# Turning tap-multiplied weights on TensorE, packing half of pair 0, and moving one tap and the bias add off VectorE

## What is computed

```python
x = x + L0(_gn(x))      # x is (16, 96, 16, 16); _gn: group norm, 32 groups of 3 channels
x = x + L1(_gn(x))
# L0: qkv = 1x1 convolution by w_qkv (288x96), then a depthwise 3x3 convolution by w_dw;
#     q and k are divided by their l2 norm over the 256 pixels; 8 heads of 12 channels:
#     attn = softmax(q k^T * temperature); out = w_proj (attn v)
# L1: s = softmax(x gate_w + gate_b) over 4 experts; the two largest are weighted by their softmax;
#     y[e] = w2[e] relu(w1[e] x + b1[e]) + b2[e]; out = sum over e of coef[e] * y[e]
#     coef[e] = sum over rank k of (expert e is at rank k for any pixel) * weight of rank k
```

## Time and profile before

| | us |
|---|---|
| median of 3 runs (168.86 to 171.39) | 170.21 |
| the profiled execution | 170.19 |
| its span, first to last instruction | 168.4 |
| PE busy | 148.9 |
| DVE busy | 144.0 |
| ACT busy | 101.4 |
| POOL busy | 45.4 |

### The profile page before, as it was taken

One profiled execution on the slowest core, in us unless ns is written; L12 is line 12 of the kernel. 1 busy time (PEld: TensorE's weight loads), 2 busy tenths in 40 slices (PEclk: granted clock), 3 DMA queues, 4 the chain that ended last, 5 costly groups with the idle time before them and its releaser, 6 DMA issues.

```text
span 168.4 us, 3554 instructions
## 1 busy us (share of the span) xinstructions
PE 148.9 (88%) x1275; PEld 118.6 (70%) x1275; DVE 144.0 (86%) x389; ACT 101.4 (60%) x227; POOL 45.4 (27%) x63
## 2 busy tenths in 40 slices
PE   0486896999998999999999899898999798999963
PEld 0476795999998999999999899675674242333322
DVE  2579999877999999999799699659779999999992
ACT  3075087565928639379399147485499768675710
POOL 5130220540514235425246225451227000000000
PEclk9999999699999999999999999999999999999999
DMA  6994305041140410503204100000000000112313
GB/s 151 226 232 103 70 0 157 6 134 26 38 124 0 133 29 0 155 9 85 76 2 117 44 0 6 0 0 2 4 0 0 0 0 0 47 47 58 90 47 93
DMA packets 8810, 9.72 MB, mean 58 GB/s; under 512 B 3640, under 2 KB 7512, under 8 KB 8792
## 3 DMA queue, kind: packets, MB, share of 16 engines
q1 hardware_dynamic: 8648, 9.25, 21.8%
q10 hardware_dynamic: 144, 0.24, 0.4%
HBM read 2.94 MB, written 1.57 MB: 27 GB/s over the span
## 4 chain that ended last, share of the span: by engine, by line
PE 44%; DVE 42%; issue 7%; DMA 2%; ACT 2%; POOL 1%; DVEq 0%; POOLq 0%
DVE v_acc L1136 9%; PE qk_ps L720 8%; PE qk_ps L722 8%; DVE h_mixed L1395 5%; PE out_ps L809 4%; DVE stats L1092 3%; PE sc_ps L774 3%; PE sc_ps L784 3%; PE qk_ps L725 3%; DMA x_sb<-in_x 2%; PE v_ps L766 2%; DVE wc L1021 2%; DVE x_sb L1403 2%; PE small_ps L826 2%; PE v_ps L969 2%
## 5 line engine op out<-in xcount | busy, mean ns | idle before, releaser
L1136 DVE SCALAR_TENSOR_TENSOR v_acc<-v_ps,v_taps,v_acc 96x576 f32<-96x576 f32 x64 | 51.8, 809 | 1.2
L720 PE MATMUL qk_ps<-w_a,x_a 128*128 128x192 f16 x243 | 46.6, 245 | 0.0
L722 PE MATMUL qk_ps<-w_b,x_b 128*128 128x192 f16 x243 | 46.5, 245 | 0.0
L720 PEld LDWEIGHTS qk_ps<-w_a,x_a 128*128 128x128 f16 x243 | 24.6, 101 | 0.2
L722 PEld LDWEIGHTS qk_ps<-w_b,x_b 128*128 128x128 f16 x243 | 23.6, 97 | 0.3
L527 ACT ACTIVATE h_mixed<-qk_ps,slope 128x512 f32<-128x512 f32 x24 | 16.9, 775 | 5.4 <-PE qk_ps L946 5.3
L725 PE MATMUL qk_ps<-w_c,x_c 96*128 96x192 f16 x81 | 20.1, 248 | 0.0
L479 ACT ACTIVATE sc_exp<-sc_qk,neg_max 96x12 f32<-96x12 f32 x16 | 4.7, 296 | 21.3 <-DVE neg_max L1175 21.3
L640 POOL TENSOR_TENSOR sq_sum<-qk_sq 128x384 f32<-128x384 f32 x8 | 8.0, 1002 | 32.8 <-ACT qk_sq L441 25.1
L1395 DVE TENSOR_TENSOR h_mixed<-h_mixed,hidden 128x512 f32<-128x512 f32 x24 | 15.0, 679 | 0.0
L1092 DVE BATCH_NORM_STATS2 stats<-x_sb 96x6 f32<-96x256 f32 x32 | 11.7, 412 | 3.0 <-DMA x_sb<-in_x 2.8
(11 more groups left out here) (200 smaller groups left out, 349.9 us busy)
## 6 DMA issues: line engine op xcount, KB each, us to landing
x_b<-x_a SPq DMA_DIRECT2D x7, 324.0 KB, 3.1
x_sb<-in_x SPq DMA_DIRECT2D x8, 192.0 KB, 4.8
out<-xs SPq DMA_DIRECT2D x7, 192.0 KB, 2.1
x_a<-x_lo SPq DMA_DIRECT2D x7, 108.0 KB, 2.7
x_b<-x_lo SPq DMA_DIRECT2D x7, 108.0 KB, 2.5
x_c<-x_lo SPq DMA_DIRECT2D x21, 36.0 KB, 1.9
wdw_all<-in_L_conv_w_dw SPq DMA_DIRECT2D x1, 648.0 KB, 6.3
w_sb<-in_L_conv_w SPq DMA_DIRECT2D x2, 144.0 KB
```

The costliest lines, as they stand in the source:

```text
L720: eng.matmul(to, window(x_a[p][:, dx, b], half, dy), w_a[:, t, :], start=(t == 0), stop=False, skip_group_check=True)
L722: mm = eng.matmul(to, window(x_b[p][:, dx, b], half, dy), w_b[:, t, :], start=False, stop=False, skip_group_check=True)
L1136: eng.scalar_tensor_tensor(out=v_acc[i % 3][:, :, :], in0=v_window(dy, dx), scalar=v_taps[:, t:t + 1], in1=v_acc[i % 3][:, :, :], op0=ALU. ...
```

## The change

- `wdw_all` and its DMA go. DVE multiplies taps into rows of w_qkv as they lie in SBUF (`combine`, taps 0 to 5; ACT's `last_taps`, 6 to 8), PE turns the 18 blocks into five PSUM banks (`turn_taps`), and ACT and DVE split them into fp16 parts from there (five groups of two taps).
- Pair 0 is normalised and rounded image by image (`normalise_first`); DVE shifts its columns. Tiles 2 and 3 of pair 0 are packed, so that SP packs the second image of pair 0 too, behind the weights.
- DVE's tap (1, 1) of v goes to ACT (`other_tap`, into `v_one`) and POOL (`add_tap`). ACT copies q and k ahead of the centre tap and squares them behind it.
- Moves: `prep_w1` of DVE and `prepare_late` of PE into pair 1, `gate(0)` and `gate(1)` behind the convolution of their pairs, `gate(2)` behind `gram(7)`, `mix_heads(7)` ahead of `first(4)`, ACT's and DVE's lists in the middle.
- Last stage: `add_bias` of DVE becomes `bias_tile` on ACT and an add on POOL; `weight(0)` gets the bank of `out_ps`; `take_u(1)` now stands ahead of `coefs(2)`; `last_second` goes by hidden tile instead of by half; a `keep_warm(3)` of PE goes.

```diff
-RELU_DVE = (2, 6, 18, 20, 22)
+RELU_DVE = (7, 18, 20, 22)
...
-        w0_ps = hid_ps[0:2]
+        w0_ps = [out_ps[:, :], hid_ps[0]]
         y_ps = [mix_ps[:, :], v_bank[0]]
+        y_last = [v_bank[1], hid_ps[1]]
...
-                eng.dma_start(x_b[p][0:C], x_a[p][0:C]).then_inc(packed[p], 16)
+
+                b = slice(1 if i == 0 else 0, 2)
+                eng.dma_start(x_b[p][0:C, :, b], x_a[p][0:C, :, b]).then_inc(packed[p], 16)
                 eng.wait_ge(lo_ready, i + 1)
-                eng.dma_start(x_a[p][C:128], x_lo[p][0:32]).then_inc(packed[p], 16)
-                eng.dma_start(x_b[p][C:128], x_lo[p][32:64]).then_inc(packed[p], 16)
+                eng.dma_start(x_a[p][C:128, :, b], x_lo[p][0:32, :, b]).then_inc(packed[p], 16)
+                eng.dma_start(x_b[p][C:128, :, b], x_lo[p][32:64, :, b]).then_inc(packed[p], 16)
                 for dx in range(3):
-                    eng.dma_start(x_c[p][32 * dx:32 * dx + 32], x_lo[p][64:C, dx]).then_inc(packed[p], 16)
+                    eng.dma_start(x_c[p][32 * dx:32 * dx + 32, b], x_lo[p][64:C, dx, b]).then_inc(packed[p], 16)
...
-            eng.dma_start(wdw_all[:, :], w_dw[0:QK].rearrange("o a b c -> (o a b c)").unsqueeze(0)
-                          .broadcast_to([C, QK * TAPS])).then_inc(in_dw, 16)
...
-            eng.wait_ge(wc_hi_set, 3)
+            eng.wait_ge(wc_hi_set, 5)
...
-            for i in range(1, PAIRS):
+            for i in range(PAIRS):
...
+            def last_taps(first, last):
+
+                eng.wait_ge(dw_set, 1)
+                for t in range(first, last):
+                    for s in range(2):
+                        a = eng.activation(wc[:, t, s * C:(s + 1) * C], wqkv_sb[:, s, :], ACT.Copy,
+                                           scale=dw_scaled[:, t, s:s + 1])
+                    a.then_inc(wc_last, 1)
+
             def high_weights(g):
                 eng.wait_ge(wc_full, g + 1)
-                eng.copy(w_a[0:C, 3 * g:3 * g + 3, :], wc[:, 3 * g:3 * g + 3, :]).then_inc(wc_hi_set, 1)
+                eng.copy(w_a[0:C, bank_taps(g), :], bank_view(g)).then_inc(wc_hi_set, 1)
...
+            def other_tap(i):
+
+                wait(eng, v_done, i - 1)
+                eng.activation(v_one[i % 2][:, :, :], v_window(1, 1), ACT.Copy, scale=v_taps[:, 8:9]).then_inc(v_one_set, 1)
...
+            def bias_tile(i):
+
+                wait(eng, x1_biased, i - 1)
+                eng.activation(b2_part[i % 2][:, :], w0_ps[i % 2][0:C, :], ACT.Identity, scale=bias_col[:, 0:1],
+                               bias=bias_col[:, 1:2]).then_inc(b2_ready, 1)
...
             square_dev(0)
-            normalise(0)
-            high_weights(0)
-            eng.copy(wv_hi[:, :], out_ps[0:C, 0:C]).then_inc(wv_set, 1)
-            shift_high(0)
-            high_weights(1)
-            high_weights(2)
+            last_taps(6, 7)
+            eng.wait_ge(wvT_ready, 1)
+            eng.copy(wv_hi[:, :], qk_ps[1][0:C, QK:QK + C]).then_inc(wv_set, 1)
+            last_taps(7, TAPS)
+            normalise_first()
+            for g in range(5):
+                high_weights(g)
 
             for i in range(PAIRS):
+                if i > 0:
+                    copy_qk(i - 1, 1)
                 centre_tap(i)
+                other_tap(i)
                 if i > 0:
-                    take_qk(i - 1, 1)
+                    square_qk(i - 1, 1)
...
             coefs(0)
-            top_exps(1)
             relu(23)
             eng.wait_ge(bias_done, 1)
             eng.copy(bias_col[:, :], small_ps[0:C, BIAS:BIAS + 2]).then_inc(bias_ready, 1)
+            top_exps(1)
+            eng.wait_ge(bias_ready, 1)
+            bias_tile(0)
             coefs(1)
-            coefs(2)
+            bias_tile(1)
             take_u(1)
-            for i in range(3, PAIRS):
+            for i in range(2, PAIRS):
                 coefs(i)
...
+            def low_first():
+                for b in range(2):
+                    eng.wait_ge(hi_mid, b + 1)
+                    eng.tensor_tensor(inner(x_lo[0], 1)[:, b], xs[0][:, b * HW:(b + 1) * HW].rearrange("c (h w) -> c h w", w=W),
+                                      inner(x_a[0], 1)[:, b], ALU.subtract).then_inc(lo_mid, 1)
...
+            def add_tap(i):
+                eng.wait_ge(v_one_set, i + 1)
+                eng.wait_ge(tap_done, 7 * (i + 1))
+                eng.tensor_tensor(v_acc[i % 3][:, :, :], v_acc[i % 3][:, :, :], v_one[i % 2][:, :, :], ALU.add).then_inc(v_done, 1)
...
             for i in range(1, PAIRS):
+                add_tap(i - 1)
                 sum_squares(i - 1)
...
+            for i in range(PAIRS):
+                eng.wait_ge(b2_ready, i + 1)
+                eng.tensor_tensor(x_sb[:, i, :], x_sb[:, i, :], b2_part[i % 2][:, :], ALU.add).then_inc(x1_biased, 1)
...
+            def prepare_v():
+                eng.wait_ge(wv_scaled_set, 1)
+                eng.wait_ge(in_c, 16)
+                eng.transpose(qk_ps[1][0:C, QK:QK + C], wv_scaled[:, :], const("ident", C)[:, 0:C]).then_inc(wvT_ready, 1)
+
+            def turn_taps(first, last):
+                for t in range(first, last):
+                    for s in range(2):
+                        at = tap_columns(t).start + s * C
+                        mm = eng.transpose(wc_ps[t // 2][0:C, at:at + C], wc[:, t, s * C:(s + 1) * C],
+                                           const("ident", C)[:, 0:C])
+                    if t % 2 == 1 or t == TAPS - 1:
+                        mm.then_inc(wc_full, 1)
...
+                if i == 0 and n < 2 or i == 1 and n == 0:
...
+                        if i == 0 and n == 0 and t % 2 == 0:
+                            eng.wait_ge(wc_hi_set, t // 2 + 1)
+                            eng.wait_ge(wc_lo_set, t // 2 + 1)
...
-                    if first == 0 and i == 1 and n == 1:
+                    if first == 0 and i == 0 and n == 2:
                         eng.wait_ge(w_packed, 16 * 5)
-                    if first == 0 and n == (1 if i == 1 else 0):
+                    if first == 0 and n == {0: 2, 1: 1}.get(i, 0):
...
+            prepare_v()
             keep_warm(3)
-            prepare_qkv()
-            keep_warm(6)
+            eng.wait_ge(wc_set, 1)
+            turn_taps(0, 3)
+            eng.wait_ge(wc_set, 2)
+            turn_taps(3, 6)
+            eng.wait_ge(wc_last, 3)
+            eng.wait_ge(wv_set, 2)
+            turn_taps(6, TAPS)
+            eng.wait_ge(norm_done, 1)
+            keep_warm(5, small_ps)
             project_v(0)
...
                 conv_taps(i, 2, 0, TAPS)
+                if i == 1:
+                    prepare_late()
                 conv_taps(i, 3, 0, 3)
-                if i >= 5:
-                    gate(i - 5, {5: 5, 6: 6, 7: 7}[i], 0)
                 if i >= 1:
                     spread_rk(i - 1)
                 conv_taps(i, 3, 3, TAPS)
-                if i == 0:
-                    prepare_late()
+                if i in (5, 6):
+                    gate(i - 5, {5: 5, 6: 6}[i], 0)
                 if i + 1 < PAIRS:
                     project_v(i + 1)
...
             first(0)
             gram(7)
+            gate(2, 7, 0, 24)
             first(1)
...
             first(3)
+            mix_heads(7)
             first(4)
-            mix_heads(7)
-            first(5)
             norm_means(7, 3)
             apply_mix(7)
             norm_vars(7)
+            first(5)
...
-                if i < 2:
-                    wait_hidden_taken(eng, HT - 4 + i)
+                if i == 0:
+                    eng.wait_ge(x1_done, PAIRS)
+                elif i == 1:
+                    wait_hidden_taken(eng, HT - 4)
                 else:
                     eng.wait_ge(coef_set, MT * (i - 1))
-                    eng.wait_ge(x1_biased, i - 1)
+                    eng.wait_ge(b2_ready, i - 1)
...
             weight(0)
-            first(23)
-            weight(1)
+            first(21)
+            first(22)
             eng.wait_ge(cols_step, 2)
             eng.matmul(small_ps[0:C, BIAS:BIAS + 2], b2_sb[:, :], slope_cols[:, :], start=True, stop=True)\
                .then_inc(bias_done, 1)
+            first(23)
+            weight(1)
...
             def last_second(i):
-                eng.wait_ge(mixed_done, MT * i + MT)
+
                 for b in range(2):
-                    t = slice(b * HW, (b + 1) * HW)
-                    to = y_ps[1 if b == 0 else 0][0:C, t]
-                    eng.wait_ge(y_taken, i - 1 + b)
-                    for m in range(MT):
-                        mm = eng.matmul(to, w2T[:, m, :], h_mixed[i % 2][:, m, t], start=(m == 0), stop=(m == MT - 1))
-                    mm.then_inc(y_done, 1)
-
-            keep_warm(3, mix_ps[:, 256:512])
+                    wait_hidden_taken(eng, HT - 1 - 2 * b)
+                for m in range(MT):
+                    eng.wait_ge(mixed_done, MT * i + m + 1)
+                    for b in range(2):
```

(38 more changed lines are left out.)

209 lines of the change are left out of this document (124 added, 85 removed).

## The result

The changed kernel takes 174.93 us (median of 4 runs, 174.4 to 175.76), the kernel before 169.54 (4 runs, 168.74 to 171.39): the ratio is 1.034, 95% interval 1.026 to 1.042. It is slower by 3.4%; forecast were 166.8 us and a range up to 170.2. The profiled execution took 174.59 us, its span 172.5.

A forecast was written before the change was run, and what follows sets the result against it. PE (44% of the chain) and DVE (42%) bound it together, read stage by stage. Stage terms, from -1.2 (pair 0) to -1.1 (last stage), summed to -3.4 us off 170.19: 166.8 us, range 163.6 to 170.2.

The forecast's parts named there:

- GpSimd's add of the bias: Last stage: POOL's 1.2 us add blocks 0.3 us of the next mix, which 0.5 us of slack takes.
- `take_u(1)`, put at 1.1 us: Last stage: it holds ACT until PE has done `second(1)`, so pair 2's coefficients come late: +1.1 us.
- the DMAs of pair 0 with the fall of the clock behind them: Pair 0: last copy lands at 21.2, PE stands 2.3 us, one fall costs 1.7; pair 1 starts at 26.3.
- the wait that `prep_w1` brings in pair 1: Pair 1: `prep_w1` takes DVE 1.65 us between taps, `add_dev` comes 0.9 us late for PE; pair's sum 0.0.
- One sign that the prediction named for being wrong as a whole: Whole kernel: wrong if the clock falls outside pair 0, or PE's start of pair 0 slips behind 14.5.
- the clock's term: Pair 0: PE's idle time is longer than 1.59 us, so one fall of the clock is taken, 1.7 us.
- the fourth rival: Pair 0: packing saves nothing, since SP's eleven issues take as long as the unpacked tiles; 168.0 us, chance 0.05.
- The tap: Pairs from 1 on: POOL's 1.3 us sum blocks `sc_qk`, charged 1.1 us; DVE's pair gets 0.3 us longer.
- The term -2.4 for pairs 5 to 7: Pairs 5 to 7: DVE has slack, gates' waits go (1.2), `gate(2)` (0.9) moves out: 33.6 us, -2.4.
- The rival of the blocked mixes: Last stage: if DVE lags ACT by 0.5 us, POOL's add blocks whole mixes, +4.4: 171.2 us, chance 0.10.
- The rival of more falls: Pair 3 and before `second(2)`: PE stands 1.4 us each; one fall gives 168.5 us, two 170.2; chance 0.17.
- The other direction: Start of kernel: DVE's `combine` holds POOL's `root(0)` up to 0.7 us; sum would be 0.4 higher, not included.

The follow-up runs named there:

- e9: Changed kernel with small matmuls of ones in all four places where TensorE stands 1.5 us or more: 172.62 us, ratio 1.018 to the kernel before.
- e7: Changed kernel with all four tiles of pair 0 unpacked, as before the change: 170.51 us, ratio 1.0045 to the kernel before.
- e6: Changed kernel with `prep_w1` moved out of pair 1 into VectorE's gap between pair 0 and pair 1: 171.17 us, ratio 1.012 to the kernel before.
- e8: Changed kernel with the tap (1, 1) of v on VectorE again, nothing of it on ScalarE and GpSimd: 173.07 us.
- e1: Changed kernel with 28 small matmuls of ones on TensorE between tiles 1 and 2 of pair 0: 172.52 us, ratio 1.013 to the kernel before.
- e5: Changed kernel with `take_u(1)` behind `coefs(2)` on ScalarE again, as in the kernel before: 171.47 us.
- e4: Changed kernel with GpSimd's add of v's ninth tap cut to 4 of each row's 288 columns: 172.5 us.
- g1: Changed kernel with TensorE's four stretches filled by matmuls of ones and GpSimd's bias add cut to 8 of 512 columns: 169.3 us, ratio 0.998.
- f3: Kernel before with one edit, `take_u(1)` ahead of `coefs(2)` on ScalarE: 172.95 us, ratio 1.022.
- f2: Changed kernel with pair 0's packing, `prep_w1`, tap and `take_u(1)` moves undone, GpSimd's bias add cut to 8 of 512 columns: 161.69 us, ratio 0.955.
- e2: Changed kernel with ten small matmuls of ones on TensorE ahead of `second(0)`: 173.83 us, ratio 1.017 to the kernel before.
- e3: Changed kernel with GpSimd's bias add cut to 8 of 512 columns: 172.63 us, ratio 1.009 to the kernel before.
- f1: Changed kernel with pair 0's packing, `prep_w1`, tap and `take_u(1)` moves undone, and the bias on VectorE again: 163.28 us, ratio 0.964.
- c1: Changed kernel with four moves undone together (pair 0's packing, `prep_w1`, the tap, `take_u(1)`): 163.71 us, ratio 0.970 to the kernel before.

## Why the prediction was wrong

The steps that failed are four terms of the sum: GpSimd's add of the bias, put at nothing; `take_u(1)`, put at 1.1 us; the DMAs of pair 0 with the fall of the clock behind them; and the wait that `prep_w1` brings in pair 1. No rival alone reaches 174.9 us; the slowest said 171.2. The profiled execution missed the forecast by 7.8 us, in rounded parts: pair 0 2.8, pair 1 1.0, pair 2 0.5, pair 3 -0.8, pairs 5 to 7 0.2, last stage 3.9, outside the span 0.3. One sign that the prediction named for being wrong as a whole came true: the clock also fell outside pair 0, in the last stage.

- **Pair 0 (-1.2 forecast, +1.5 measured).** The end of the rounding (13.0) and of the unpacked tiles (18.7) were right. The DMAs were mis-sized: the last issue began 0.7 us later than summed, one issue having taken 1.02, and landed after 2.55, not 1.9, us. TensorE stood 3.85 instead of 2.3 us (in other profiles 2.3 to 4.2) and went on at 22.69 instead of 21.2: 1.5 of the 2.8 us. The rest is the clock's term: I took one row's 3.4 us as the length of a fall, and it was twice that. e9 gives 26.23 at full clock, close to the forecast's 26.3, which had a fall in it and too short a wait: that agreement is luck. Whether packing pays at all was the fourth rival, with a chance of 0.05 and a price of 168.0 us; it was the right question, since without packing pair 1 starts at 23.7 (e7).
- **Pair 1 (0.0 forecast, +0.95).** I had the new wait at 0.9 us; it was 1.86. `prep_w1` was priced at 1.65, which it takes with nothing of GpSimd beside it; here its `w_top` stood 0.9 us beside GpSimd's `x_lo`, a lock of the kind that I had charged to `sc_qk` alone. e6 shows the wait gone with the step, e8 that 0.6 of it was ScalarE's second tap. In all five other profiles with the same wait (e1 to e5) a fall comes with it, and the pair takes 14.3 us.
- **Pair 2 (+0.8 forecast, +1.2 measured).** The wait for `low_w1` came as said, 0.8 us long; e6 has 0.5.
- **The tap.** The mechanism was right: GpSimd's sum took 1.40 (1.3 forecast) and blocked `sc_qk` for 0.9 to 1.2 us, but in four pairs, not in seven. In the changed kernel one such pair and one without it:

```profile
40.73 1.40 POOL L720 TENSOR_TENSOR v_acc<-v_acc,v_one 96x576 f32<-96x576 f32 x1 [0.58 <-DVE v_acc L1261]
40.98 1.19 DVE L1297 TENSOR_TENSOR sc_qk<-sc_k,q_fac 96x24 f32<-96x24 f32 x1
...
52.86 0.18 DVE L1297 TENSOR_TENSOR sc_qk<-sc_k,q_fac 96x24 f32<-96x24 f32 x1
```

  In e4 it was worth 0.8 us, in pairs 4 to 7; what it is worth in pair 2 without a fall in pair 1 is open. Pair 3, which was forecast 0.5 longer, got 0.3 shorter; pair 4 was right. The term -2.4 for pairs 5 to 7 was right (-2.2), and the tap has no part in it: with the tap back they take 33.42 (e8). That it comes from the gates, as the sum had it, no run shows.
- **Last stage (-1.1 forecast, +2.9 measured).** The frame was right: with neither loss it takes 27.56, a gain of 2.3 where -2.2 stood in the sum. `take_u(1)` was put at +1.1 and costs 1.6 to 1.9 (g1, f3). GpSimd's add was put at nothing, covered by 0.5 us of slack; it costs 1.8 even in the right order (e5 against f2). Together they cost another 1.7, which a sum of terms cannot show. The rival of the blocked mixes was the right mechanism, with 4.4 us for it near the 3.5 measured (e9 against g1), and had 0.10. Its condition was VectorE's lag behind ScalarE, and what stood against it (0.5 us of slack) was worked out for a pipeline in step, while `take_u(1)`, in the same paragraph, was what would make VectorE late.
- **The clock.** With single stretches filled (e1, e2) falls came in other places; with all filled (e9) the profile has none. The 4.4 us by which the profiled executions differ are 3.0 of waits (e9 against 168.7, the kernel before at full clock), 2.9 lost to the clock in the changed kernel, less the 1.5 that the fall cost the kernel before (170.19 against 168.7). The rival of more falls had 0.17. Of its places, pair 3 never showed one, and behind `second(2)`'s wait, 1.6 us, the changed kernel's profile has none, though six others do (e1, e3, e4, e6, e7, e8). It missed pair 1, the longer fall in pair 0, and `second(0)`: the `keep_warm(3)` that went stood there, not ahead of `second(2)`.

The Trainium skill, "SBUF — State Buffer", section "Who interferes with whom", was cited for the lock, and by it the blocking goes either way. The trace agrees: the add at 144.02 took 1.62 us, and the one at 151.43, of the same shape, 1.27. The same section of the Trainium skill says that a `tensor_scalar` can take part too when it runs in a two-port mode; `top_den`, a TENSOR_SCALAR with one input tensor, was 0.16 us with the bias on VectorE (f1) and 1.24 beside the add (c1 and the changed kernel), which agrees.

The other direction, which the prediction set at 0.4 us for `root(0)` but left out of the sum, is there too. In the changed kernel (rows 1 and 2) `combine` is running when GpSimd's `root(0)` begins, which takes 1.09 us; in the kernel before (row 3) it took 0.70:

```profile
7.79 0.74 DVE L1146 TENSOR_TENSOR wc<-wqkv_sb,dw_scaled 96x576 f32<-96x576 f32 x1
8.02 1.09 POOL L739 TENSOR_TENSOR rstd<-var_eps,minus_half 96x2 f32<-96x2 f32 x1 [4.91 <-DVE var_eps L1242]
...
7.97 0.70 POOL L649 TENSOR_TENSOR rstd<-var_eps,minus_half 96x2 f32<-96x2 f32 x1 [5.00 <-DVE var_eps L1118]
```

The rounding ended at 13.0 all the same, so this 0.4 us is no part of the miss. One slip of the sum: four packed tiles of 21 matmuls at 0.08 us are 6.7 us, not 6.9; no term hangs on it.

Open: why one of the eleven issues takes long, and why the last DMA of pair 0 lands after 1.8 us in one execution and 2.55 in another, which together put its landing between 21.8 and 23.3 us; and why the same stretch brings a fall in some executions and none in others. No run was made for either.

## What to carry over

In this kernel, work moved to GpSimd was not off VectorE's path wherever VectorE's instruction had two inputs in SBUF, nor beside `top_den`, which has one: list what VectorE does in the time of each moved instruction, every place of it, and charge the whole of it, above all behind a step that makes VectorE late. Where an engine will stand for a new wait, ask first whether the work that brings the wait is worth it at full clock (here it cost 2.5 us), then price the half clock by the worst stretch seen. Terms that make the same engine late can cost more together than apart (5.1 against 3.4 us here): price them together.

## What the runs showed that was not expected

- The clock's answer to the same wait differs between executions. For the DMAs of pair 0, TensorE stood 2.3 to 2.65 us and kept its clock (e2, e4, e5). In others it stood 3.85 and 3.94 us and was at half for 6.8 us (the changed kernel, e6), and 4.1 to 4.2 us and was at half for 3.4 (e3, e8). In f3 it was at half for 10.2 us in pair 0, behind a wait of 1.05 us at most.
- Instructions of 0.16 us (`w_top` on 128x3, `top_den` on 128x16) took 1.05 and 1.24 us beside a GpSimd instruction on 96x512, and ended within 0.03 us of it: what these lost was GpSimd's remaining time, however small they were themselves.
- Eleven issues from SP took 6.95 us to the start of the last, one of them 1.02 where its neighbours took 0.6. This was no accident of one execution: in all ten profiles in which pair 0 is packed (the changed kernel, e1 to e6, e8, e9, g1) one issue of the last six is long, 1.02 to 1.94 us (e8), and the last begins at 19.97 to 20.87. With the five weight issues alone (e7, f1 and the kernel before) none takes over 0.67.
